# Waits for keys only where a group of keys is new, and query-key products summed by TensorE in the last five steps

## The reference, cut to what matters

```python
q, k, v = split_heads(x @ Wq + bq), split_heads(x @ Wk + bk), split_heads(x @ Wv + bv)   # 16 heads of 8
attn_logits = einsum('hbsd,hbtd->hbst', q, k) * scale          # 16 queries, 16 keys
gates = sigmoid(attn_logits); pos = cumsum from the last key; pos = min(pos, 124)
attn_logits += logits of q @ pos_emb, read between floor(pos) and ceil(pos)
out = softmax(attn_logits) @ v;  return out @ Wo + bo
```

## Time and profile before

| | us |
|---|---|
| median of 3 runs | 2865.48 |
| the profiled execution, its own time | 2860.1 |
| its span, first to last instruction | 2858.4 |
| busy in the span: PE, DVE, ACT, POOL | 2352.3, 1702.4, 1169.0, 777.0 |
| mean granted TensorE clock | 0.885 |

### The profile page before, as it was taken

How to read it: one execution, slowest core, us unless ns; L and a number is a source line. 1 busy time by engine, 2 the same in 40 slices (tenths; PEclk the granted TensorE clock), 3 DMA queues, 4 the chain that set the end, 5 groups by cost and what they waited for, 6 DMA issues and landing times. The chain is left out here.

```text
span 2858.4 us, 41081 instructions
## 1 busy us (share of the span) xinstructions
PE 2352.3 (82%) x14101; PEld 1418.2 (50%) x14101; DVE 1702.4 (60%) x3205; ACT 1169.0 (41%) x2549; POOL 777.0 (27%) x1431
## 2 busy tenths in 40 slices
PE   3788899999999999998979798898888986455554
PEld 1233345454555544455656565666566754233333
DVE  3455555555555555411268666876677768788883
ACT  0244455555555555543424333443434343222222
POOL 3223333433334434322212222132213121110000
PEclk9788799999999999988989898989889997666666
DMA  5322322222232223000000000000000000000000
GB/s 138 72 60 50 68 65 56 65 52 69 46 76 46 61 61 76 2 16 30 30 30 16 19 4 34 33 17 19 5 34 1 34 5 4 0 4 4 4 4 8
DMA packets 87826, 101.41 MB, mean 35 GB/s; under 512 B 11065, under 2 KB 82369, under 8 KB 83521
## 3 DMA queue, kind: packets, MB, share of 16 engines
q1 hardware_dynamic: 80770, 94.42, 13.5%
q10 hardware_dynamic: 6848, 4.36, 0.6%
HBM read 68.35 MB, written 29.62 MB: 34 GB/s over the span
## 5 line engine op out<-in xcount | busy, mean ns | idle before, releaser
L774 DVE TENSOR_REDUCE maxima<-scores 128x2 f32<-128x1024 f32 (+3 forms) x512 | 421.9, 824 | 538.2 <-PE scores L645 533.1
L493 PEld LDWEIGHTS experts_bank<-w,hidden 128*128 128x128 f32 x4096 | 536.0, 197 | 153.6 <-issue 150.2
L493 PE MATMUL experts_bank<-w,hidden 128*128 128x128 f32 x4096 | 562.6, 282 | 0.0
L882 ACT ACTIVATE probs<-turned 128x512 f32<-128x512 f32 (+3 forms) x1024 | 393.2, 435 | 151.9 <-issue 98.4
L970 POOL TENSOR_SCALAR_AFFINE_SELECT probs<-probs 128x256 f32<-128x256 f32 x512 | 212.4, 415 | 657.0 <-ACT probs L882 656.7
L481 ACT ACTIVATE hidden<-rest_bank 128x512 f32<-128x512 f32 x308 | 183.2, 595 | 454.1 <-issue 270.4
L475 PE MATMUL rest_bank<-xe,w 128*128 128x512 f32 x616 | 346.3, 651 | 24.5 <-POOL xe L464 19.4
L1691 POOL TENSOR_SCALAR shift<-mv2b 128x4 f32<-128x4 f32 x48 | 39.4, 820 | 967.6 <-DVE mv2b L1427 967.6
L1438 DVE TENSOR_TENSOR prod<-q,kv 128x2048 f32<-128x2048 f32 x64 | 146.1, 2284 | 158.5 <-ACT kv L1595 156.9
L481 ACT ACTIVATE hidden<-hidden_bank 128x512 f32<-128x512 f32 x204 | 121.6, 596 | 288.3 <-issue 229.8
L663 PE MATMUL turned<-q_stack,k_stack 51*128 51x512 bf16 (+3 forms) x1024 | 196.0, 319 | 27.7 <-ACT probs L882 16.3
(11 more groups left out here) (237 smaller groups left out, 3324.5 us busy)
## 6 DMA issues: line engine op xcount, KB each, us to landing
mask_all<-mask_scratch SPq DMA_DIRECT2D x32, 1024.0 KB, 5.1
stack_q<-parts_q SPq DMA_DIRECT2D x96, 128.0 KB, 2.5
stack_k<-parts_k SPq DMA_DIRECT2D x96, 128.0 KB, 2.4
q_stack<-stack_q SPq DMA_DIRECT2D x32, 384.0 KB, 5.8
k_stack<-stack_k SPq DMA_DIRECT2D x32, 384.0 KB, 9.4
x<-in_L_attn_batch_dram SPq DMA_DIRECT2D x16, 256.0 KB, 5.4
w<-in_L_ffn_W_dram ACTq DMA_DIRECT2D x16, 256.0 KB, 3.0
out_dram<-x SPq DMA_DIRECT2D x16, 256.0 KB, 2.3
```

Source lines behind the costliest of these rows:

```text
L493: mm = pe.matmul(bank[:, n * P:(n + 1) * P], m.hidden[:, q % 4, n * P:(n + 1) * P], t.w2[:, k, :], start=False, stop=(k == E * F - 1), ski ...
L774: dve.tensor_reduce(mx[:, w % 2, :, p, qt], s_bank[:, :, 0:(qt + 1) * P], AX.X, ALU.max)\
L882: act.activation(probs[:, 2 * p + e, KEYS_AT[kt]:KEYS_AT[kt] + width], st_bank[:, e, 0:width], ACT.Exp, scale=SCALE).then_inc(s_exp, 1)
```

## The change

In step i with i not a multiple of 4, DVE does not wait for this step's keys (they belong to the next block) and does logits 0 at its start. In steps 0, 4, 8 and 12 the wait stays. The keys' statistics come before the experts' sum unless the keys are of the very group that is summed (`sum_is_for_keys`, step 0 alone); POOL's and ACT's positions follow. The queries of group i + 1 are made at position 19 of step i, in the bank of the weight sums, with semaphores of their own. The last addition of a group moves behind values 0 of the next step. From step 11 on (`LONE`), DVE writes the products of query and keys to one of two unused buffers, and PE adds the 8 numbers of each head with products by the identity: 2 halves of keys x 8 places, 128 columns each, into a pair of banks; tanh and L1458 read these banks. These sums stand at PE's positions 12, 14, 16 and 17.

```diff
+LONE = 11
+
+
+def group_of(keys):
+    return ROWS_FIRST + ORDER.index(divmod(keys, R))
...
+        self.queries = 0 if keys == 2 else attend + 1 if attend is not None and attend < GROUPS - 1 else None
+
+    def sum_is_for_keys(self):
+        return self.summed is not None and self.keys is not None and self.keys % R > 0 and group_of(self.keys) == self.summed
...
+        products = [u[:, :, :].rearrange("p e n -> p (e n)").rearrange("p (t d) -> p t d", d=D) for u in (m.xe, m.hidden)]
+        summed_logits = pair[:, :, :].rearrange("p b n -> p (b n)")
+        half_logits = [pair[:, n, :].rearrange("p (t g h) -> p g t h", g=G, h=H) for n in range(2)]
...
         def pe_queries(pe, i):
-            pe.wait_ge(s_m2_read, before_m2(i) + 1)
+            if i > 1:
+                pe.wait_ge(s_wsum_read, i - 1)
             for j in range(G):
-                mm = pe.matmul(m2[:, j * P:(j + 1) * P], kept[:, i % R, j * P:(j + 1) * P], t.w_at[:, 0:D], start=True, stop=True)
-            mm.then_inc(s_m2, 1)
+                mm = pe.matmul(w_bank[:, j * P:(j + 1) * P], kept[:, i % R, j * P:(j + 1) * P], t.w_at[:, 0:D], start=True, stop=True)
+            mm.then_inc(s_q, 1)
...
             pe.wait_ge(s_p, i)
+            pe.wait_ge(s_q_read, min(i + 1, GROUPS))
...
+        def pe_logits(pe, i, j):
+
+            c = G * (i - LONE) + j
+            pe.wait_ge(s_prod, c + 1)
+            by_place = products[c % 2].rearrange("p t (h d) -> p d t h", d=HD)
+            for n in range(2):
+                for d in range(HD):
+                    mm = pe.matmul(half_logits[n][:, j, :, :], t.ident[:, :], by_place[:, d, n * S // 2:(n + 1) * S // 2, :],
+                                   start=(d == 0), stop=(d == HD - 1))
+            mm.then_inc(s_prod_read, 1)
...
+                if k == 19 and step.queries is not None:
+                    pe_queries(pe, step.queries)
                 if step.attend is not None:
-                    if k == 3:
-                        pe_queries(pe, i)
                     if k in (4, 6, 9, 14):
                         pe_kinks(pe, i, (4, 6, 9, 14).index(k))
...
+                if step.attend is not None and i >= LONE and k in (12, 14, 16, 17):
+                    pe_logits(pe, i, (12, 14, 16, 17).index(k))
...
             if j == 0:
-                dve.wait_ge(s_m2_read, before_m2(i) + 2)
+                dve.wait_ge(s_q_read, i + 1)
             keys = keys_of(i)[:, :, 0:D]
+            if i >= LONE:
+                c = G * (i - LONE) + j
+                if c >= 2:
+                    dve.wait_ge(s_prod_read, c - 1)
+                dve.tensor_tensor(products[c % 2], q[:, j, :].unsqueeze(1).broadcast_to([P, S, D]), keys, ALU.mult)\
+                   .then_inc(s_prod, 1)
+                return
...
+            from_logits = summed_logits if i >= LONE else logits[:, :, :, :].rearrange("p t g h -> p (t g h)")
+            own(dve.scalar_tensor_tensor(acc[:, :, :, :].rearrange("p t g h -> p (t g h)"), from_logits, SCALE,
...
+            sum_first, early = step.sum_is_for_keys(), attend and finish and i % R > 0
+            if early:
+                v_logits(dve, own_m, i, 0)
+            if sum_first:
                 m.v_sum_stats(dve, step.summed)
-            elif keys is not None:
+                m.v_sum_add(dve, step.summed)
+            if keys is not None:
+                if keys % R > 0:
+                    dve.wait_ge(m.s_x1, group_of(keys) + 1)
                 v_keys_stats(dve, keys)
+            if step.summed is not None and not sum_first:
+                m.v_sum_stats(dve, step.summed)
             if finish:
                 v_weight_sums(dve, own_q, i)
-            if finish:
                 v_values(dve, own_q, i, 0)
-            if finish:
+                if i > 1:
+                    v_last_add(dve, i - 1, before_m2(i - 1))
                 v_values(dve, own_q, i, 1)
-            if step.summed is not None:
-                m.v_sum_add(dve, step.summed)
-                dve.wait_ge(m.s_x1, step.summed + 1)
-            if step.summed is not None and keys is not None:
-                v_keys_stats(dve, keys)
             if step.gates is not None:
                 m.v_row_stats(dve, step.gates)
             if finish:
                 v_values(dve, own_q, i, 2)
-            if keys is not None:
-                dve.wait_ge(s_m1_read, fill_of["high", keys] + 1)
+            if step.summed is not None and not sum_first:
+                m.v_sum_add(dve, step.summed)
+            if attend and i % R == 0:
+                dve.wait_ge(s_m1_read, fill_of["high", i + R - 1] + 1)
             if finish:
                 dve.wait_ge(s_vsum, 4 * (i - 1) + 3)
-            if attend:
+            if attend and not early:
                 v_logits(dve, own_m, i, 0)
             if finish:
                 v_values(dve, own_q, i, 3)
...
+                if not attend:
+                    v_last_add(dve, i, n2)
...
-                if k == 5 and step.summed is not None:
+                if k == (5 if step.sum_is_for_keys() else 8) and step.summed is not None:
                     m.a_sum_scale(act, step.summed)
...
-                if k == 4 and attend:
-                    a_queries(act, i)
+                if k == 20 and step.queries is not None:
+                    a_queries(act, step.queries)
...
+                    if i >= LONE:
+                        await_(act, passed["scalar"], s_prod_read, G * (i - LONE + 1))
+                    else:
+                        await_(act, passed["scalar"], s_lg, i + 1)
+                    act.activation(pos[:, :, :, :].rearrange("p t g h -> p (t g h)"), summed_logits if i >= LONE
+                                   else logits[:, :, :, :].rearrange("p t g h -> p (t g h)"), ACT.Tanh, scale=0.5 * SCALE).then_inc(s_tanh, 1)
...
-                if k == 2 and step.summed is not None:
+                if k == (2 if step.sum_is_for_keys() else 5) and step.summed is not None:
                     m.p_sum_root(pool, step.summed)
-                if k == 5 and keys is not None:
+                if k == (5 if step.sum_is_for_keys() else 2) and keys is not None:
```

More of the change, by code:

```diff
@@ L1250, in sb @@
             return ctx.enter_context(nc.sbuf_tensor(name, shape, dt))
-        banks = [ctx.enter_context(nc.psum_tensor(f"rest_bank{i}", [P, 512], F32)) for i in range(7)]
-        h_bank, m1, k_bank, y2_bank, m2, w_bank = banks[0:2], banks[2], banks[3], banks[4], banks[5], banks[6]
+        pair = ctx.enter_context(nc.psum_tensor("pair_bank", [P, 2, 512], F32))
+        banks = [ctx.enter_context(nc.psum_tensor(f"rest_bank{i}", [P, 512], F32)) for i in range(5)]
+        h_bank, m1, k_bank, y2_bank, m2, w_bank = [pair[:, 0, :], pair[:, 1, :]], *banks
         y_bank = m.y_bank
@@ L1374, in pe_step @@
             finish, last = step.finish is not None, step.attend is None
-            n2 = before_m2(i) - (1 if last else 0) if finish else None
+            n2 = before_m2(i) if finish else None
             for k in range(E * F + 2):
+                if k == 19 and step.queries is not None:
+                    pe_queries(pe, step.queries)
                 if step.attend is not None:
-                    if k == 3:
-                        pe_queries(pe, i)
                     if k in (4, 6, 9, 14):
@@ L1457, in v_positions @@
             dve.wait_ge(s_k_read, 4 * i + 5)
-            own(dve.scalar_tensor_tensor(acc[:, :, :, :].rearrange("p t g h -> p (t g h)"),
-                                         logits[:, :, :, :].rearrange("p t g h -> p (t g h)"), SCALE,
+            from_logits = summed_logits if i >= LONE else logits[:, :, :, :].rearrange("p t g h -> p (t g h)")
+            own(dve.scalar_tensor_tensor(acc[:, :, :, :].rearrange("p t g h -> p (t g h)"), from_logits, SCALE,
                                          kinks[:, NPOS:, :, :].rearrange("p t g h -> p (t g h)"), ALU.mult, ALU.add))
@@ L1491, in v_weight_sums @@
             dve.wait_ge(s_wsum, i)
-            own(dve.reciprocal(wsum[:, :], w_bank[:, 0:G * H]))
-            dve.wait_ge(s_vec_q, own.value())
+            dve.reciprocal(wsum[:, :], w_bank[:, 0:G * H]).then_inc(s_wsum_read, 1)
+            dve.wait_ge(s_wsum_read, i)
             flat = acc[:, :, :, :].rearrange("p t g h -> p t (g h)")
@@ L1535, in v_step @@
             attend, finish, keys = step.attend is not None, step.finish is not None, step.keys
-            n2 = before_m2(i) - (0 if attend else 1) if finish else None
-            if step.summed is not None:
+            n2 = before_m2(i) if finish else None
+            sum_first, early = step.sum_is_for_keys(), attend and finish and i % R > 0
+            if early:
+                v_logits(dve, own_m, i, 0)
+            if sum_first:
                 m.v_sum_stats(dve, step.summed)
-            elif keys is not None:
+                m.v_sum_add(dve, step.summed)
+            if keys is not None:
+                if keys % R > 0:
```

(24 more changed lines are left out.)

9 lines of the change are left out of this document (5 added, 4 removed).

## The result

The changed kernel takes **2876.36 us** (median of six runs, 2874.17 to 2879.99). The kernel before took 2864.7 beside it (six runs), a ratio of 1.0042 with a 95% interval of 1.0029 to 1.0055: a little slower, by more than chance explains. The profiled execution took 2874.17 us with a span of 2872.4, 14.0 more than before. The forecast of 2794 us was wrong in size and in sign.

What follows compares the result with a forecast made beforehand. Neither engine was full: PE and DVE run in order and wait for each other. Gains of 60.6 + 6.8 + 3.7 = 71 us off 2860.1 give 2789, and 5.4 for the median gives 2794 us; range 2760 to 2832.

Steps and rivals of the forecast that it cites:

- (a): Steps 2, 3, 4, 6, 7, 8, 10: keys' statistics right after the softmax end PE's stall at the turned keys, 32.1 us gained.
- (b): Same seven steps: PE's half clock after the stall at the turned keys goes, 16.8 us gained.
- (c): Steps 1 to 10 but 4 and 8: early first logits end PE's wait for the fourth weighted values, 13.2 us gained.
- (f): Last addition moved behind the first values: gain 0; removing DVE's wait for the keys in itself: 0.
- (e): Steps 2, 3, 6, 7, 10: DVE's early logits and statistics before the reciprocal delay the first mixture, 10.5 us lost.
- (d): Steps 1 to 10: the queries leave the part from weight sums to projection for position 19, 9 us gained.
- Steps 11 to 16: Logits sums on PE at 3.5 us each; step 11 gains 8.0 us, later steps lose some, 3.7 us gained in all.
- C: Rival on PE's logits sums: 7 us each, by low clock or stepped reading, 2861 us; chance 0.08.
- D: Rival on PE's logits sums: half-pace reading and low clock together, some 9.5 us each, 2915 us; chance 0.06.
- break-even of 7.05 us a sum: Steps 11 to 15, 20 logits sums on PE: from 7.05 us a sum on, the forecast gain of 71 us is gone.
- identity products over 5 us: Sign in the profile that the forecast is wrong: PE's 32 identity products were to take 3.5 us.

Runs made afterwards that it cites:

- pairs run: The changed kernel with DVE writing the products in runs of two floats and PE reading at a step of two floats: 2815.53 us, ratio 0.9803.

## Why the prediction was wrong

**(a) and (b), the keys' statistics**: right in their sum. Forecast 48.9 us in steps 1 to 10 and the 7.50 of step 11; undone, they cost 43.7 and 10.7. The parts were each off by some: PE's idle time in steps 1 to 10 grew by 21.7 us, where (a) had 32.1, and its busy time by 22.0, where (b) had 16.8 for the low clock.

**(c), 13.2 us for the fourth mixture**: the stall went, and as a stall its price was right (17.8 us of it in steps 1 to 10 with the wait, 3.4 without), but the early first logits got the credit. The removal of the wait does it, which (f) had put at 0, and it is worth 16 to 19 us there.

**(e), minus 10.5 us**: the sign is right, the size 4 us short. Early logits in steps 1 to 10 cost 14.6 us (887.7 against 873.1), and 15.0 by the medians (2797.49 - 2782.45). The first mixture is later as (e) says: in step 3 it starts 9.0 us after L1343 without them and 11.5 with them, 2.6 later, where (e) had 2.0 to 2.1. But little of that is the stall for DVE's values that (e) names:

```profile
1652.56 1.13 PE L475 MATMUL pair_bank<-xe,w 128*128 128x512 f32 x2 [1.74 <-ACT hidden L481]
1657.76 1.94 PE L1365 MATMUL rest_bank<-ident,hidden 128*128 128x128 f32 x16 [0.58 <-DVE hidden L1541]
```

The larger stall, 1.74 us, is for the experts' relu on ACT. Over steps 1 to 10 PE is busy 8.1 us longer with early logits (790.3 in the run without PE's sums against 782.1 in the one without the wait) and idle 6.6 longer. Why ACT is late there, and what lowers the pace, stays open.

**(d), the queries**: not tried by itself. The sum of (a) to (f) was 60.6 us, and 59.8 were found, which is closer than the terms deserve. From weight sums to projection, (a) and (b) undone cost 43.5 us of it (48.9 forecast), and (c), (e) and the wait undone together 3.1 (2.7 forecast, as two errors of the same size cancel). Some 13 us are left for (d), forecast at 9, and for what the terms do to each other.

**Steps 11 to 16**: the step that failed is "the nearest row, with contiguous columns, gives 3.5", taken as the price of a logits sum. It is 7.4 to 7.5 us. I had its cause in hand, and gave it 0.14 in rivals C and D, because a row nearby looked like evidence; but the row had another form of reading, and so said nothing on it. That is rival C by the reading alone, at 7.4 to 7.5 us instead of its 7; what D added to it, the low clock, did not count, since a stepped sum took nearly the same at 0.77. My break-even of 7.05 us a sum gives, at 7.43, 71 - 20 x 3.93, a loss of 8 us, 2873 us, and 2876 was measured. This is near, but in part by luck: it takes each us of a sum in full, and the runs give 68 us for 20 sums that were 3.65 us longer, 0.93 us for each, much as C had it (66 for 3.6). The rest was another error of the same forecast. Of the 79 us, 68 are the pace (518.3 against 450.1 in the pairs run), and 11 my count of the steps at the right pace: steps 13 to 15 at 75.3 on the average where I had 72.7 (some 3 us of these 8 are the two sums at low clock), step 12 at 78.5 where I had 77.1, and step 16 2.9 us longer instead of 0.7 (1.7 longer without PE's sums).

**What the profile was to show**: turned keys without a stall, 42.5 us from weight sums to projection in step 6 and the part behind it unchanged came true; "identity products over 5 us" was the sign of being wrong, and stood there.

**Left open.** The untouched first half ends between 1256.38 and 1273.16 us in the profiled executions of these kernels (DVE's last instruction of it), and step 1 starts between 1462.80 and 1477.92; nothing here says why, and it can move medians by some us.

## What to carry to other kernels

Before work is moved to another engine, look at how that engine will have to read it: a row with the same shape but another access pattern is no price. Where no row has the pattern, put the break-even beside both ends and ask for a small measurement of that one instruction: here 3.8 or 7.5 us a sum decided between 2816 (the run with pairs) and 2876. And a change in two parts is to be timed in two parts: one of these won 2.5% by itself, and the other lost some 80 us. A count of PE's time alone isn't enough either: at the right pace, too, the sums stood in front of work that everything waits for, and cost 12 us against leaving them on DVE (450.1 against 437.9).

## What the runs showed of the hardware

- PE reads f32 columns at full pace at a step of one or two floats, and at half at four or eight: 3.7 to 3.9 and 7.5 to 7.6 us for 32 instructions of 128 columns, all at a granted clock of 1.00.
- At the slow pace the clock hardly mattered as far as it fell here: 7.54 us from start to start at a mean granted clock of 0.77, 7.43 at 1.00. The same 32 instructions reading at a step of two floats took 5.33 us at a mean of 0.71 and 3.79 at 1.00 (the run with the sums behind the projection).
- DVE pays for single floats too, and not for runs of two: a product of 128x2048 f32 takes 2.26 to 2.29 us written side by side or in runs of two, and 3.65 to 3.79 in single floats 1 KB apart. The Trainium skill (Vector Engine (DVE) Microarchitecture Reference, "Measured stream behaviour on trn2", the paragraph "The SBUF access granule: adjacent pairs") states full rate for runs of two or more adjacent 4-byte words, and for another instruction 1.71 ns a column against 1.054 when the output hops at every element, an estimate from it of 1.6 times; the trace agrees, by 1.6 to 1.7 times. For reading at a step of eight floats the ratio here is 1.75 (3.97 us).
- Summed logits in PSUM cost their readers nothing: tanh takes 1.02 us from there and 1.06 from SBUF, and DVE's `acc` 1.22 us from there (L1496) and 1.23 from SBUF (the run without PE's sums).
